# In the full attentions the value projections change places with the turns of normed rows

## The chip, the cores and the metric

The kernel runs on one core of a Trainium2 chip. The metric is the time of one execution in microseconds on the device, the median of three runs. A profile was taken of one more execution.

## The reference, cut to what matters

The reference sends x, 32 sequences of 128 rows with 256 columns, through four layers. Each layer adds an attention over a context to x and then a feed-forward net. Layers 0, 1 and 3 have the same form of attention, the "full attention" here (layer 2 has a windowed one):

```
xn = layernorm(x)                                   # rows of 256
q = xn @ Wq.T + bq;  k = ctx @ Wk.T + bk;  v = ctx @ Wv.T + bv      # 16 heads of 16
scores = (q . k * tau + delta) / 4                  # per head, 128 x 128
a = softmax(scores);  x = x + (a . v) @ Wo.T + bo
```

The feed-forward nets (a routed one, one with rounded weights, product keys, a top-2 one) and the windowed attention are not touched by the change.

## The kernel before

`attention` runs three times (a0, a1 and a3 in the names, for layers 0, 1 and 3). A tile t is one sequence of 128 rows with all 16 heads; four tiles make a group g, and u is the tile's place in its group (t = 4g + u, 32 tiles, 8 groups). Queries and keys are projected for a whole group (512 columns), half of the features at a time; values for two tiles at a time; the normed rows of two tiles at a time are turned (transposed by TensorE against the identity), since the query projection wants features on the partitions.

Each engine has its program written out in order; semaphores tie them together. Nothing plans or reorders. TensorE's program for a tile t (function `tile` under `@block.tensor`) is:

1. `scores` of tile t+1 (L517, 32 matmuls on 32 rows each), which wait until the exponentials of tile t-1 have left the score banks;
2. `values_over_sums` of tile t-1 (L560);
3. `first_filler`: one piece of projection or turning for a later group;
4. `turned_scores` of tile t (L534, 32 matmuls), which wait until VectorE has taken both maxima of tile t+1 (L686) out of the score banks, and has added the maxima of tile t to its queries;
5. `turned_maxima` of tile t+1 (L544);
6. `second_filler`: another such piece;
7. `output_rows` of tile t-2 (L570).

The score banks are thus used in turn by the scores (read by VectorE's maxima) and the turned scores (read by ScalarE's exponentials, `exps`, L342).

The fillers, by u: 0, queries of the next group (L490), first half in the first filler and second half in the second; 1, keys of the next group (L475) in the same way; 2 and 3, in the first filler the turns of the normed rows of the group after next (`columns`, L484, four transposes), in the second filler a value projection (`values`, L498, eight matmuls). Groups 6 and 7 have no group after next, so their first filler is empty in u = 2 and 3; group 7 has of the values only those of u = 2. All fillers write one PSUM bank, `ps_m`, and each waits until ScalarE has evicted what the filler before wrote there.

ScalarE's program for a tile: the eviction of the second filler of the tile before, the eviction of output rows (L349), in some tiles the norm of two tiles of the group after next (L318) or work on the rounded weights of layer 1 (`integers`, in a1), the eviction of the first filler (values L337, turned rows L324), and the exponentials. VectorE: maxima, turning back and dividing (L701, L708), adding maxima (L694), statistics of finished rows (L143, L145); in a0 and a1 it takes the statistics of later rows of x as well in tiles 0 to 7. GpSimd multiplies keys by tau (L433) around u = 1 and 2 and adds rows into x (L440, L444). SP's queue loads the context of group g+2 when values and keys of group g are done.

Of the kernel before, what the change touches and what calls it, by code (L numbers as in the profile page):

```python
# [17 lines left out]
KC = D // P  # L18
# [5 lines left out]
GROUPS = TILES // G  # L24
# [177 lines left out]
def attention(nc, keep, tag, w, inputs, ctxT, following, load_first=False, integers=None, arrival=None, spins=(0, 0)):  # L202

    with ExitStack() as ctx:
# [3 lines left out]
        def sem(name):  # L208
            return keep["semaphore"](f"{tag}_{name}")

        def bank(name):
            return ctx.enter_context(nc.psum_tensor(f"{tag}_ps_{name}", [P, 512], F32))
# [29 lines left out]
        ps_o, ps_m, ps_y, ps_z = bank("o"), bank("m"), bank("y"), bank("z")  # L242
# [6 lines left out]
        k_full, k_taken, k_ready = sem("k_full"), sem("k_taken"), sem("k_ready")  # L249
        xn_ready, xt_full, xt_taken = sem("xn_ready"), sem("xt_full"), sem("xt_taken")  # L250
        q_full, q_taken = sem("q_full"), sem("q_taken")
        v_full, v_taken = sem("v_full"), sem("v_taken")
# [44 lines left out]
        def _(act):  # L297
            def keys(g, c, src):
                n = g * KC + c
                act.wait_ge(k_full, n + 1)  # L300
                if n >= 2:
                    act.wait_ge(k_ready, n - 1)
                for f in range(2):
                    ins = act.activation(kraw[:, c, f, :], src, ACT.Identity, scale=marks[:, 2 + f:3 + f],
                                         bias=bk4[:, f, c:c + 1])
                ins.then_inc(k_taken, 1)
# [15 lines left out]
            def columns(g, n, src):  # L322
                act.wait_ge(xt_full, g * 2 + n + 1)
                act.activation(xnT[:, :, n * 256:(n + 1) * 256], src.rearrange("p (k n) -> p k n", k=KC),  # L324
                               ACT.Copy).then_inc(xt_taken, 1)

            def queries(g, s, c, src):
                act.wait_ge(q_full, g * KC + c + 1)
                for f in range(2):
                    ins = act.activation(qT[:, s, f, c, :], src, ACT.Identity, scale=marks[:, f:f + 1],  # L330
                                         bias=bq4[:, f, c:c + 1])
                ins.then_inc(q_taken, 1)

            def values(g, s, n, src):
                act.wait_ge(v_full, g * 2 + n + 1)
                pairs = v[:, s, n * HEADS:(n + 1) * HEADS, :].rearrange("p a (b e) -> p a b e", b=3)
                act.activation(pairs[:, :, 0:3:2, :], src.rearrange("p (a b e) -> p a b e", b=2, e=DK),  # L337
                               ACT.Copy).then_inc(v_taken, 1)
# [12 lines left out]
            def first_filler(g, u):  # L351
                s, m = g % 2, ps_m[:, :]
                if u == 0 and g + 1 < GROUPS:
                    queries(g + 1, 1 - s, 0, m)
                elif u == 1 and g + 1 < GROUPS:
                    keys(g + 1, 0, m)
                elif u >= 2 and g + 2 < GROUPS:
                    columns(g + 2, u - 2, m)

            def second_filler(g, u):  # L360
                s, m = g % 2, ps_m[:, :]
                if u == 0 and g + 1 < GROUPS:
                    queries(g + 1, 1 - s, 1, m)
                elif u == 1 and g + 1 < GROUPS:
                    keys(g + 1, 1, m)
                elif u == 2:
                    values(g, s, 1, m)
                elif u == 3 and g + 1 < GROUPS:
                    values(g + 1, 1 - s, 0, m)

            def tile(g, u):
                t = g * G + u
                if t:
                    second_filler((t - 1) // G, (t - 1) % G)
                if t >= 3:
                    outputs(t - 3)
                if arrival and t == Arrival.LATE:
                    deviations(2)
                if g + 2 < GROUPS and u in (1, 2):
                    norm(g + 2, u - 1)  # L380
                if integers and g == 3 and u < 3:
                    integers.magnitudes(act, u)
                if integers and 0 <= t - ROUND_FROM < 12:
                    integers.rounded(act, 2 * (t - ROUND_FROM))
                    integers.rounded(act, 2 * (t - ROUND_FROM) + 1)
                first_filler(g, u)
                exps(t)
# [82 lines left out]
        def _(pe):  # L470
            def keys(g, s, c, dst):
                if c == 0:
                    wait_context(pe, g, s)
                for k in range(KC):
                    ins = pe.matmul(dst, wk[:, k, c * P:(c + 1) * P], ctx_t[:, s, k, :], start=(k == 0),  # L475
                                    stop=(k == KC - 1))
                ins.then_inc(k_full, 1)

            def columns(g, n, dst):
                pe.wait_ge(xn_ready, g * 2 + n + 1)  # L480
                for u in (2 * n, 2 * n + 1):
                    for k in range(KC):
                        at = k * 256 + (u % 2) * P
                        ins = pe.transpose(dst[:, at:at + P], xn[:, u, k * P:(k + 1) * P], ident[:, :])  # L484
                ins.then_inc(xt_full, 1)

            def queries(g, c, dst):
                pe.wait_ge(xt_taken, g * 2 + 2)
                for k in range(KC):
                    ins = pe.matmul(dst, wq[:, k, c * P:(c + 1) * P], xnT[:, k, :], start=(k == 0),  # L490
                                    stop=(k == KC - 1))
                ins.then_inc(q_full, 1)

            def values(s, n, dst):
                for u in range(2):
                    at = (2 * n + u) * P
                    for k in range(KC):
                        ins = pe.matmul(dst[:, u * D:(u + 1) * D], ctx_t[:, s, k, at:at + P], wv[:, k, :],  # L498
                                        start=(k == 0), stop=(k == KC - 1))
                ins.then_inc(v_full, 1)  # L500
# [72 lines left out]
            def columns_taken(g, n):  # L573
                pe.wait_ge(xt_taken, g * 2 + n + 1)

            def first_filler(g, u):
                m, more = ps_m[:, :], g + 1 < GROUPS
                if u == 0 and more:
                    if g == 0:
                        columns_taken(0, 1)  # L580
                    else:
                        pe.wait_ge(v_taken, 2 * g + 1)
                    queries(g + 1, 0, m)
                elif u == 1 and more:
                    pe.wait_ge(q_taken, (g + 1) * KC + 2)
                    keys(g + 1, (g + 1) % 2, 0, m)
                elif u == 2 and g + 2 < GROUPS:
                    pe.wait_ge(k_taken, (g + 1) * KC + 2)
                    columns(g + 2, 0, m)
                elif u == 3 and g + 2 < GROUPS:  # L590
                    pe.wait_ge(v_taken, 2 * g + 2)
                    columns(g + 2, 1, m)

            def second_filler(g, u):
                s, m, more = g % 2, ps_m[:, :], g + 1 < GROUPS
                if u == 0 and more:
                    pe.wait_ge(q_taken, (g + 1) * KC + 1)
                    queries(g + 1, 1, m)
                elif u == 1 and more:
                    pe.wait_ge(k_taken, (g + 1) * KC + 1)  # L600
                    keys(g + 1, 1 - s, 1, m)
                elif u == 2:
                    if g + 2 < GROUPS:
                        columns_taken(g + 2, 0)
                    elif more:
                        pe.wait_ge(k_taken, (g + 1) * KC + 2)
                    else:
                        pe.wait_ge(v_taken, 2 * g + 1)
                    values(s, 1, m)
                elif u == 3 and more:  # L610
                    if g + 2 < GROUPS:
                        columns_taken(g + 2, 1)
                    else:
                        pe.wait_ge(v_taken, 2 * g + 2)
                    values(1 - s, 0, m)

            def tile(g, u):
                t = g * G + u
# [2725 lines left out]
```

## Time and profile before

| what | value |
|---|---|
| median of 3 runs | 3050.51 us (3050.44 to 3053.91) |
| profiled execution | 3049.06 us, its span 3047.2 us |
| TensorE matmuls (PE) | 2832.8 us busy, 93% of the span |
| VectorE (DVE) | 2095.7 us, 69% |
| ScalarE (ACT) | 1158.2 us, 38% |
| GpSimd (POOL) | 984.4 us, 32% |

The span reaches from the first to the last instruction; the execution's time has 1.86 us around it. The three full attentions lie at about 28 to 290, 826 to 1090 and 2598 to 2858 us, so they make up a quarter of the span; the long stretch between the second and the third belongs to the product keys. Busy shares are means over stages with different limits, so they say little on one stage; a stage is read from its own timeline and from what its waits end on. In a timeline, instructions of one line that follow one another stand in one row, with the count behind the x; "us" reaches from the first start to the last end, and as matmuls overlap, the next row starts before that end.

### The profile page before, as it was taken

Reading aid. Unit: us, or ns where it says so; the run is one execution under the profiler, and the core shown is the slowest. Engines: PE = TensorE matmul, PEld = TensorE weight load, DVE = VectorE, ACT = ScalarE, POOL = GpSimd, SP = SyncE. Lnnn points to the kernel's source line nnn. Section 1 sums busy time; section 2 is a strip of 40 time slices with the busy share of each in tenths; the row PEclk is TensorE's granted clock in tenths of the full one; section 3 lists DMA queues with packets and bytes.
Section 4 is the critical chain, followed back from the end, with each engine's and each line's share of the span. In section 5 each row is a group of like instructions: output and inputs, shape, how many; then the busy total and the mean of one; then the engine's idle time right before and its main releaser. Section 6 shows DMA issues by size and latency. Waiting matters only on the chain. (4 is left out here: it accounts for less than half of the span.)

```text
span 3047.2 us, 60068 instructions
## 1 busy us (share of the span) xinstructions
PE 2832.8 (93%) x23998; PEld 2131.4 (70%) x23998; DVE 2095.7 (69%) x6103; ACT 1158.2 (38%) x1771; POOL 984.4 (32%) x1024
## 2 busy tenths in 40 slices
PE   8997999999899979897999999999999997999798
PEld 5665766566566656576888888888888885666565
DVE  5766355200277789666999899999999997567534
ACT  5654221222366669554222222222222220655532
POOL 1332000133223322000444444444444444223255
PEclk9999999999999999999999999999999997999899
DMA  4011120234401000402120000000000001100077
GB/s 143 30 43 32 55 74 21 65 100 127 128 29 43 16 12 1 145 22 94 51 82 5 5 5 5 5 6 5 5 5 5 5 5 43 60 29 30 17 228 227
DMA packets 112675, 152.90 MB, mean 50 GB/s; under 512 B 14608, under 2 KB 92688, under 8 KB 112016
## 3 DMA queue, kind: packets, MB, share of 16 engines
q1 hardware_dynamic: 100608, 126.89, 12.5%
q0 software_dynamic: 10752, 21.11, 2.7%
q8 instruction: 194, 3.18, 0.4%
q10 hardware_dynamic: 1040, 1.05, 0.1%
q14 instruction: 81, 0.66, 0.1%
HBM read 102.76 MB, written 46.27 MB: 49 GB/s over the span
## 5 line engine op out<-in xcount | busy, mean ns | idle before, releaser
L2226 POOL TENSOR_TENSOR pk_hisig<-pk_hihot,pk_sigs 128x512 f16<-128x512 f16 x512 | 520.3, 1043 | 660.1 <-DVE pk_hihot L2502 658.6
L2324 PE MATMUL pk_ps<-X,dw_downT 128*128 128x256 f32 x2048 | 479.0, 385 | 0.0
L2370 PE MATMUL pk_ps<-ew_up,pk_act_h 128*128 128x256 f32 x2048 | 459.1, 383 | 1.7 <-DVE pk_act_h L2490 1.7
L2370 PEld LDWEIGHTS pk_ps<-ew_up,pk_act_h 128*128 128x128 f32 x2048 | 388.9, 191 | 56.9 <-issue 2.0
L2324 PEld LDWEIGHTS pk_ps<-X,dw_downT 128*128 128x128 f32 x2048 | 380.2, 191 | 59.7 <-issue 14.8
L2234 ACT ACTIVATE pk_act_h<-pk_ps 128x512 f32<-128x512 f32 x256 | 152.8, 597 | 544.3 <-PE pk_ps L2324 544.3
L2503 DVE TENSOR_TENSOR pk_lohot<-pk_iota_h,pk_ps 128x1024 f16<-128x1024 f16 x256 | 310.1, 1212 | 0.0
L686 DVE TENSOR_REDUCE a_mx<-a_ps_s 128x8 f32<-128x1024 f32 x192 | 226.3, 1221 | 116.4 <-PE a_ps_s L517 101.9
L342 ACT ACTIVATE a_pT<-a_ps_s 128x2048 f32<-128x2048 f32 x96 | 180.2, 1877 | 122.0 <-PE a_ps_s L534 121.9
L2490 DVE TENSOR_TENSOR pk_act_h<-pk_act_h,pk_ps 128x512 f32<-128x512 f32 x256 | 171.3, 679 | 61.3 <-PE pk_ps L2354 61.3
L444 POOL TENSOR_TENSOR X<-a_y,a_tmp 128x256 f32<-128x256 f32 x96 | 69.8, 727 | 405.8 <-ACT a_y L349 404.4
L534 PE MATMUL a_ps_s<-a_qT,a_kT 32*128 32x128 f32 x3072 | 112.7, 283 | 59.2 <-DVE a_mx L686 59.2
L534 PEld LDWEIGHTS a_ps_s<-a_qT,a_kT 32*128 32x128 f32 x3072 | 94.4, 186 | 104.4 <-DVE a_mx L686 103.8
L2354 PEld LDWEIGHTS pk_ps<-pk_hisig,pk_lohot 128*128 128x128 f16 x4096 | 140.7, 99 | 37.1 <-DVE pk_act_h L2490 11.4
L2354 PE MATMUL pk_ps<-pk_hisig,pk_lohot 128*128 128x64 f16 x4096 | 145.7, 195 | 17.4 <-POOL pk_hisig L2226 7.2
L1512 DVE TENSOR_TENSOR ro_tmp<-ro_ps,ro_b 128x256 f32<-128x256 f32 x28 | 11.9, 424 | 190.0 <-PE ro_ps L1473 190.0
L517 PEld LDWEIGHTS a_ps_s<-a_kT,a_qT 32*128 32x128 f32 x3072 | 94.5, 186 | 46.5 <-issue 35.8
L694 DVE TENSOR_TENSOR a_qT<-a_ps_z,a_qT 128x512 f32<-128x512 f32 x96 | 66.4, 691 | 86.3 <-PE a_ps_z L544 86.3
L517 PE MATMUL a_ps_s<-a_kT,a_qT 32*128 32x128 f32 x3072 | 112.7, 283 | 11.7 <-ACT a_pT L342 8.2
L2502 DVE TENSOR_TENSOR pk_hihot<-pk_iota_h,pk_ps 128x256 f16<-128x256 f16 x256 | 105.6, 412 | 20.4 <-ACT pk_sigs L2275 20.4
L2313 PE MATMUL pk_ps<-pk_wm,pk_xb 128*128 128x512 f32 x256 | 117.0, 600 | 1.6 <-issue 1.6
L1145 PE MATMUL sh_ps<-sh_xnT,sh_w 128*128 128x512 f32 x256 | 117.7, 606 | 0.7 <-issue 0.7
(419 smaller groups left out, 5172.3 us busy)
## 6 DMA issues: line engine op xcount, KB each, us to landing
ro_w<-in_L_W SPq DMA_DIRECT2D x16, 1024.0 KB, 7.2
sent<-pk_zero SPq DMA_DIRECT2D x3, 3072.0 KB, 11.1
mo_xb<-sent SPq DMA_DIRECT2D x36, 256.0 KB, 4.4
made<-mo_yb SPq DMA_DIRECT2D x36, 256.0 KB, 3.8
i_ctx_t<-in_ctxT SPq DMA_DIRECT2D x16, 512.0 KB, 3.6
i_side<-in_side SPq DMA_DIRECT2D x16, 512.0 KB, 4.6
row_dram<-sh_row SPq DMA_DIRECT2D x8, 512.0 KB, 3.0
sum_dram<-sh_new SPq DMA_DIRECT2D x8, 512.0 KB, 2.9
```

The lines of the kernel that those rows point to most:

```text
L342: act.activation(pT[:, :, :], ps_s[:, :, :, :].rearrange("p r h n -> p (r h) n"), ACT.Exp).then_inc(p_taken, 1)
L517: ins = pe.matmul(ps_s[:, r, 2 * c + f, :], qT[row, s, f, c, at], kT[row, s, f, c, at], start=True, stop=True, skip_group_check=True)
L534: ins = pe.matmul(ps_s[:, r, 2 * c + f, :], kT[row, s, f, c, at], qT[row, s, f, c, at], start=True, stop=True, skip_group_check=True)
L686: dve.tensor_reduce(mx[:, :, 0:4, c:c + 1].rearrange("p f r a -> p r (f a)"), ps_s[:, :, 2 * c:2 * c + 2, :], AX_X, ALU.max).then_inc(max_ ...
L1145: ins = pe.matmul(main.bank(f"up{c}")[:, :], w1[:, k, c * P:(c + 1) * P], xnT[:, k, g * GT:(g + 1) * GT], start=(k == 0), stop=(k == KC - 1))
L2226: ins = pool.tensor_tensor(hisig[:, buf, n, :, :, :], hi, sig2.broadcast_to([P, TP, 2, ECH]), ALU.mult)
L2234: hid.take(act.activation(act_h[:, p % 2, 2 * c:2 * c + 2, :], hid.bank(f"h{c}")[:, :].rearrange("p (c n) -> p c n", c=2), ACT.Gelu), f"h{c}")
L2324: ins = pe.matmul(hid.bank(f"h{c}")[:, j * 2 * P:(j + 1) * 2 * P], downT[:, k, e * P:(e + 1) * P], XT[:, p, k, :], start=(k == 0), stop=(k ...
L2354: ins = pe.matmul(wts.bank(f"w{b}")[:, j * 2 * ECH:(j + 1) * 2 * ECH], lohot[:, buf, j, :], hisig[:, buf, n, j, :, :].rearrange("p r c -> ...
L2370: ins = pe.matmul(tail.bank("y")[:, 0:D], act_h[:, p % 2, c, s * P:(s + 1) * P], up[:, c, :], start=(c == 0), stop=(c == ECH - 1))
L2490: wts.take(dve.tensor_tensor(hv, hv, wts.bank(f"w{b}")[:, :].rearrange("p (j c) -> p c j", c=ECH), ALU.mult), f"w{b}")
L2503: ins = dve.tensor_tensor(lohot[:, buf, :, :], *against(0, P))
```

## The change

In tiles with u = 2 and u = 3 the two fillers change places: the value projection stands ahead of the turned scores, and the turns of normed rows behind the turn of the maxima. ScalarE's evictions change places with them. The waits for `ps_m` are rewritten for the new order: a value projection now waits for the filler of the tile before, the turns for the eviction of the values (`v_taken`). What is computed, and the number of instructions, stays. Layer 2's attention and the nets stay as they were.

```diff
--- before.py
+++ after.py
@@ -354,8 +354,10 @@
                     queries(g + 1, 1 - s, 0, m)
                 elif u == 1 and g + 1 < GROUPS:
                     keys(g + 1, 0, m)
-                elif u >= 2 and g + 2 < GROUPS:
-                    columns(g + 2, u - 2, m)
+                elif u == 2:
+                    values(g, s, 1, m)
+                elif u == 3 and g + 1 < GROUPS:
+                    values(g + 1, 1 - s, 0, m)
 
             def second_filler(g, u):
                 s, m = g % 2, ps_m[:, :]
@@ -363,10 +365,8 @@
                     queries(g + 1, 1 - s, 1, m)
                 elif u == 1 and g + 1 < GROUPS:
                     keys(g + 1, 1, m)
-                elif u == 2:
-                    values(g, s, 1, m)
-                elif u == 3 and g + 1 < GROUPS:
-                    values(g + 1, 1 - s, 0, m)
+                elif u >= 2 and g + 2 < GROUPS:
+                    columns(g + 2, u - 2, m)
 
             def tile(g, u):
                 t = g * G + u
@@ -574,22 +574,25 @@
                 pe.wait_ge(xt_taken, g * 2 + n + 1)
 
             def first_filler(g, u):
-                m, more = ps_m[:, :], g + 1 < GROUPS
+                s, m, more = g % 2, ps_m[:, :], g + 1 < GROUPS
                 if u == 0 and more:
-                    if g == 0:
-                        columns_taken(0, 1)
-                    else:
-                        pe.wait_ge(v_taken, 2 * g + 1)
+                    columns_taken(g + 1 if g else 0, 1)
                     queries(g + 1, 0, m)
                 elif u == 1 and more:
                     pe.wait_ge(q_taken, (g + 1) * KC + 2)
                     keys(g + 1, (g + 1) % 2, 0, m)
-                elif u == 2 and g + 2 < GROUPS:
-                    pe.wait_ge(k_taken, (g + 1) * KC + 2)
-                    columns(g + 2, 0, m)
-                elif u == 3 and g + 2 < GROUPS:
-                    pe.wait_ge(v_taken, 2 * g + 2)
-                    columns(g + 2, 1, m)
+                elif u == 2:
+                    if more:
+                        pe.wait_ge(k_taken, (g + 1) * KC + 2)
+                    else:
+                        pe.wait_ge(v_taken, 2 * g + 1)
+                    values(s, 1, m)
+                elif u == 3 and more:
+                    if g + 2 < GROUPS:
+                        columns_taken(g + 2, 0)
+                    else:
+                        pe.wait_ge(v_taken, 2 * g + 2)
+                    values(1 - s, 0, m)
 
             def second_filler(g, u):
                 s, m, more = g % 2, ps_m[:, :], g + 1 < GROUPS
@@ -599,20 +602,9 @@
                 elif u == 1 and more:
                     pe.wait_ge(k_taken, (g + 1) * KC + 1)
                     keys(g + 1, 1 - s, 1, m)
-                elif u == 2:
-                    if g + 2 < GROUPS:
-                        columns_taken(g + 2, 0)
-                    elif more:
-                        pe.wait_ge(k_taken, (g + 1) * KC + 2)
-                    else:
-                        pe.wait_ge(v_taken, 2 * g + 1)
-                    values(s, 1, m)
-                elif u == 3 and more:
-                    if g + 2 < GROUPS:
-                        columns_taken(g + 2, 1)
-                    else:
-                        pe.wait_ge(v_taken, 2 * g + 2)
-                    values(1 - s, 0, m)
+                elif u >= 2 and g + 2 < GROUPS:
+                    pe.wait_ge(v_taken, 2 * g + u)
+                    columns(g + 2, u - 2, m)
 
             def tile(g, u):
                 t = g * G + u
```

## Rows read from the trace of the kernel before

**Rows 1.** The page, part 5, the scores and turned scores on TensorE.

```profile
L534 PE MATMUL a_ps_s<-a_qT,a_kT 32*128 32x128 f32 x3072 | 112.7, 283 | 59.2 <-DVE a_mx L686 59.2
...
L517 PE MATMUL a_ps_s<-a_kT,a_qT 32*128 32x128 f32 x3072 | 112.7, 283 | 11.7 <-ACT a_pT L342 8.2
```

**Rows 2.** The maxima's tile: who waited for it (us in all, times).

```profile
  PE a_ps_s L534: 59.2, 54
```

**Rows 3.** TensorE's timeline, first attention: start, us, line, times, [idle before].

```profile
124.20 1.17 PE L517 MATMUL a_ps_s<-a_kT,a_qT 32*128 32x128 f32 x32
125.31 1.08 PE L560 MATMUL a_ps_o<-a_pT,a_v 128*32 128x128 f32 x32
126.32 0.66 PE L484 MATMUL a_ps_m<-ident,a_xn 128*128 128x128 f32 x4
127.86 1.17 PE L534 MATMUL a_ps_s<-a_qT,a_kT 32*128 32x128 f32 x32 [0.88 <-DVE a_mx L686]
128.96 0.44 PE L544 MATMUL a_ps_z<-ident,a_mx 128*128 128x128 f32 x2
129.24 1.89 PE L498 MATMUL a_ps_m<-a_wv,i_ctx_t 128*128 128x256 f32 x8
130.97 1.03 PE L570 MATMUL a_ps_y<-a_wo,a_oT 128*128 128x256 f32 x4
131.92 1.17 PE L517 MATMUL a_ps_s<-a_kT,a_qT 32*128 32x128 f32 x32
...
134.04 1.98 PE L490 MATMUL a_ps_m<-a_xnT,a_wq 128*128 128x512 f32 x4
135.95 1.17 PE L534 MATMUL a_ps_s<-a_qT,a_kT 32*128 32x128 f32 x32
```

**Rows 4.** The same stretch in the timeline of all engines.

```profile
125.44 2.36 DVE L686 TENSOR_REDUCE a_mx<-a_ps_s 128x8 f32<-128x1024 f32 x2 [1.63 <-PE a_ps_s L517]
...
129.10 1.88 ACT L342 ACTIVATE a_pT<-a_ps_s 128x2048 f32<-128x2048 f32 x1 [1.49 <-PE a_ps_s L534]
...
131.35 0.18 DVE L145 BATCH_NORM_AGGREGATE MV<-a_bst 128x2 f32<-128x6 f32 x1
...
137.40 1.87 ACT L342 ACTIVATE a_pT<-a_ps_s 128x2048 f32<-128x2048 f32 x1
```

**Rows 5.** Timeline of all engines, last group of the first attention.

```profile
264.63 1.17 PE L534 MATMUL a_ps_s<-a_qT,a_kT 32*128 32x128 f32 x32 [1.47 <-DVE a_mx L686]
...
265.87 1.88 ACT L342 ACTIVATE a_pT<-a_ps_s 128x2048 f32<-128x2048 f32 x1 [4.40 <-PE a_ps_s L534]
...
267.80 1.17 PE L517 MATMUL a_ps_s<-a_kT,a_qT 32*128 32x128 f32 x32 [0.76 <-ACT a_pT L342]
```

**Rows 6.** TensorE's timeline, tiles 2 and 3 of the first and second attention.

```profile
47.99 1.17 PE L517 MATMUL a_ps_s<-a_kT,a_qT 32*128 32x128 f32 x32
...
52.67 1.17 PE L534 MATMUL a_ps_s<-a_qT,a_kT 32*128 32x128 f32 x32 [1.91 <-DVE a_mx L686]
...
54.05 3.58 PE L498 MATMUL a_ps_m<-a_wv,i_ctx_t 128*128 128x256 f32 x8
...
66.20 1.17 PE L517 MATMUL a_ps_s<-a_kT,a_qT 32*128 32x128 f32 x32
...
845.70 1.17 PE L517 MATMUL a_ps_s<-a_kT,a_qT 32*128 32x128 f32 x32
...
850.40 1.17 PE L534 MATMUL a_ps_s<-a_qT,a_kT 32*128 32x128 f32 x32 [1.92 <-DVE a_mx L686]
...
862.23 1.17 PE L517 MATMUL a_ps_s<-a_kT,a_qT 32*128 32x128 f32 x32
```

**Rows 7.** Busy time by stretches: length, engines (PE first), PEclk, DMA share, GB/s.

```profile
55.00:56.00 1.00, 1.00 (x4) 0.81 (x3) 0.97 (x4) 0.79 (x1) 0.00 (x0) 0.50 0.00 0
```

**Rows 8.** Timeline of all engines, around the product of keys on POOL.

```profile
146.06 2.36 POOL L433 TENSOR_TENSOR a_kT<-a_kraw,i_side 128x1024 f32<-128x1024 f32 x1 [3.88 <-ACT a_kraw L304]
...
146.55 2.15 DVE L708 TENSOR_TENSOR a_rows_o<-a_turned,a_rden 128x256 f32<-128x256 f32 x1
```

## The prediction

> **What bounds the kernel now.** I read the page first, part 5: the turned scores (L534) and the scores (L517) of the three full attentions are the matmuls ahead of which TensorE stands idle, and the turned scores wait for VectorE's maxima [rows 1]. The view of the maxima's tile then says how often: 54 waits, 59.2 us in all [rows 2]. 54 is 45 + 9: per attention 15 tiles whose first filler is the turns of normed rows or nothing while values come later (u=2 and u=3 of groups 0 to 6, u=2 of group 7), and 3 others (tile 0 and the first two of group 7). So I read one such tile in TensorE's timeline [rows 3]. Scores start at 124.20, values over sums at 125.31, the turns at 126.32; the turned scores can't start before 127.86, with 0.88 idle; then come the value projections, 1.73 until the next matmul, and output rows; the next scores start at 131.92. The tile takes 7.72 us, of which TensorE's instructions fill all but that gap. The reader is to see in the tile behind it that queries, 1.91 us long in the same place, leave no gap at all.
>
> What else could set the tile's end is read in the same stretch with all engines [rows 4]: the maxima run 125.44 to 127.80, which is what the gap ends on; the exponentials start at 129.10, 1.24 behind the start of the turned scores, and take 1.88, to 130.98. The next scores need them, and start 0.94 later, so now they are hidden behind value projections and output rows. The last group shows what happens where they are not [rows 5]: turned scores at 264.63, exponentials 265.87 to 267.75, scores at 267.80 after 0.76 idle. From the start of the turned scores to the next scores nothing is shorter than 1.24 + 1.88 + 0.05 = 3.17.
>
> **The change part by part.** No instruction is added or removed; in u=2 and u=3 the 8 value matmuls and the 4 turns (and their two ScalarE evictions) change places. Queues other than PE and ACT keep their order. SP's load of the group after next waits for the second value projection of a group, which now ends about 2.9 us sooner (4.0 behind the scores, not 6.9): at nothing, as a load can only come earlier by it.
>
> First gap. Ahead of the turned scores TensorE now has 1.11 + 1.01 of scores and values over sums, then the value projections. Those take 1.73 up to output rows [rows 3]; up to 32-row matmuls it may be more: four output matmuls, half as many columns, take 0.95 up to the scores (131.92 less 130.97), 0.09 over half of 1.73. The bounds are 1.73 and the 1.91 of queries, which stream as many columns (4 x 512 for 8 x 256) in just this place. I take 1.73 + 0.09 = 1.82, since its rows are the same matmul form. The turned scores then start 2.12 + 1.82 = 3.94 behind the scores, not 3.66, and no longer wait for the maxima (3.66), which have 0.28 to spare.
> The Trainium skill's "TensorEngine Tiling (Array Packing)", section Key Properties, says that changing the tiling mode drains TensorE. A whole drain would hold the turned scores until the last value matmul's end (1.89 behind the first start, as the row of these eight matmuls has it), and the sum below would be 37 x 0.07 = 2.6 us less; the row with output matmuls ahead of scores shows a switch at 0.09, so the trace agrees that it costs, and with less than a whole drain.
>
> Second gap. Behind the turned scores (1.10, from 127.86 to 128.96) TensorE now has the turn of the maxima (0.28), four turns (4 x 0.14 by the two of the maxima, 0.56) and output rows (0.95): 2.89. That no longer covers 3.17, so the exponentials set the end of the tile, with 0.28 idle ahead of the scores. This is where a part of the gain stops: without it the tile would be 6.83 long.
>
> The tile: 3.94 + 3.17 = 7.11 against 7.72, a gain of 0.61 (0.70 and 0.52 at the bounds of the switch).
>
> ScalarE. The eviction of the values (0.60) now stands ahead of the exponentials. It can start when the values are done (about 4.05) and is over at 4.65; the exponentials can't start before 3.94 + 1.24 = 5.18, so nothing. The turns wait for it as they share the bank; they come at about 5.3. The eviction of the turns goes behind the exponentials, over some 0.6 into the next tile, where its bank is wanted at 2.12. If the cover is gone, the exponentials follow the eviction directly, as behind the queries [rows 4]: 137.40 is 1.45 behind 135.95, not 1.24, and each tile loses 0.21.
>
> VectorE. It ends its tile 3.67 behind the start of the turned scores (131.53 less 127.86) [rows 4], so at 7.61; its next maxima may start 1.24 into the next tile, at 8.35. Hidden, with 0.74 left. In tiles 2, 3, 6 and 7 of the first two attentions it carries statistics as well. In tile 2 the maxima come late, and the turned scores start 4.70 behind the scores in the second attention [rows 6]. They stay there, values or not; what follows is now 3.17 instead of 4.06. The next tile is as the others, 7.11. So tiles 2 and 3 take 4.70 + 3.17 + 7.11 = 14.98 against 862.23 - 845.70 = 16.53: a gain of 1.55. For tiles 6 and 7, with the same load on VectorE, I take the same.
>
> The clock. In the first attention tiles 2 and 3 take 66.20 - 47.99 = 18.21 [rows 6], 1.68 more than the same tiles of the second: the eight value matmuls last 3.58 instead of 1.89, and the granted clock is 0.50, the 1.2 GHz level [rows 7]. TensorE had just been idle for 1.91; it would now be idle for 0.76 (4.70 less 3.94). I take the fall as gone: 1.55 + 1.68 = 3.23; the ends are 1.55 and 3.23. That a gap of 1.92 in the second attention brought no fall makes this uncertain.
>
> The sum: of 45 tiles 37 are regular, 37 x 0.61 = 22.6; the two pairs of the second attention and one of the first, 3 x 1.55 = 4.65; the first pair of the first, 3.2. Together 30.5 us. The profiled execution took 3049.06 around a span of 3047.2, so 3018.6; the median of the runs is 1.45 above it, 3050.51, so 3020.0. With the switch at its ends: 37 x 0.52 + 7 = 26 and 37 x 0.70 + 8.5 = 34.
>
> **The rivals.**
> The exponentials late. The eviction ahead of them delays each by up to 0.21, or the switch costs more than its bound. For it: behind queries they start at the eviction's end. Against: two evictions of 0.73 there, one of 0.60 here. 37 x 0.40 + 8 x 0.7 = 20 us: 3030.
> No second limit. If output rows and turns stretched over the exponentials or these came sooner, the tile would be 6.83: 45 x 0.88 = 40 us: 3011. Against: rows 5 show that the scores start 0.05 behind the exponentials.
> VectorE takes the place. Its product with the reciprocals takes 2.15 instead of about 0.4 where GpSimd's product of keys lies beside it [rows 8]. If the shifted tiles met that in u=2 or u=3, VectorE would be 1.74 later, 1.0 over its slack of 0.74, and a tile would take some 0.7 longer than forecast, all of its gain: 3050, no change. Against: the keys' product in u=2 is started by the tile before, and the product with the reciprocals comes later than now, not sooner.
> The clock falls more often. The tiles lose a gap of 0.88 and get one of 0.28 at another place; should the half level then be granted in tiles where it is not now, each fall costs 1.69 by the 3.58 against 1.89. From 18 falls on (30.5 / 1.69) the change doesn't gain; at one in each attention group, 24, it is 3060, slower by 0.3%. Against: the last group, with gaps of 1.47 and 0.76 in each tile, keeps its durations (1.17 for the scores [rows 5]).
> The Trainium skill's "TensorE: Matmul & The Clock Gate", section Part 1, says that activity releases the throttle and idling brings it back, which speaks against this rival too; the fall in the first attention agrees, the second, without a fall behind the same gap, doesn't settle it.
>
> **How the numbers follow.** The forecast 0.77; exponentials late 0.13; no second limit 0.02; VectorE 0.05; clock 0.03. A change of under 0.2% (6.1 us) is about what a measurement of this kernel can't tell from none. Faster is 0.77 + 0.13 + 0.02 = 0.92; same 0.05; slower 0.03. The range is 3015.0 to 3030.0: below, the switch at its cheap end and 1 us for what is left (34 + 1.5); above, the exponentials late. What it leaves out is less than 0.2.
>
> **What would show it.** In the changed profile: regular tiles of 7.1 from scores to scores; value matmuls (L498) between values over sums and turned scores; the idle time of L534 behind the maxima down from 59.2 to some 13 (the 9 other waits and the first tile of four pairs); L517 waiting for the exponentials in some 45 tiles more than now, about 0.3 each; tile 2 of the first attention with eight value matmuls at 1.89. Wrong would be: turned scores that still wait for the maxima in regular tiles, exponentials over 1.3 behind the turned scores, or scores that start more than 0.1 behind the exponentials.

## The result, and the profile after

The changed kernel takes 3027.18 us (median of 4 runs, 3022.56 to 3029.39) against 3052.21 (4 runs, 3050.44 to 3055.29): ratio 0.9917, 95% interval 0.9906 to 0.9929, 25 us less. The forecast was 30.5 us less than the 3050.51 known then, so 3020.0, in a range from 3015.0 to 3030.0. The profiled execution took 3026.22 us around a span of 3024.4.

The page's part 5 for the two matmuls that [rows 1] shows (columns as there; the program's lines behind L600 have moved up by 8, those of the scores haven't):

```profile
L517 PE MATMUL a_ps_s<-a_kT,a_qT 32*128 32x128 f32 x3072 | 114.1, 285 | 28.4 <-ACT a_pT L342 24.9
...
L534 PE MATMUL a_ps_s<-a_qT,a_kT 32*128 32x128 f32 x3072 | 112.7, 283 | 12.0 <-DVE a_mx L678 12.0
```

The idle time ahead of the turned scores fell from 59.2 to 12.0 us, and that ahead of the scores rose from 11.7 to 28.4: 47 us went in one place, and 17 came back in another. Who waited for the maxima, in the view of their tile, answers [rows 2]:

```profile
  PE a_ps_s L534: 12.0, 12
```

12 waits for 54: of the 45 changed tiles only the first tiles of the four pairs with additional statistics still wait, 0.57 or 0.29 each. TensorE's timeline of a regular tile, which answers [rows 3] (start, us, line, count, idle before):

```profile
119.72 1.17 PE L517 MATMUL a_ps_s<-a_kT,a_qT 32*128 32x128 f32 x32 [0.33 <-ACT a_pT L342]
120.82 1.08 PE L560 MATMUL a_ps_o<-a_pT,a_v 128*32 128x128 f32 x32
121.83 1.99 PE L498 MATMUL a_ps_m<-a_wv,i_ctx_t 128*128 128x256 f32 x8
123.76 1.17 PE L534 MATMUL a_ps_s<-a_qT,a_kT 32*128 32x128 f32 x32
...
125.14 0.60 PE L484 MATMUL a_ps_m<-ident,a_xn 128*128 128x128 f32 x4
125.57 1.03 PE L570 MATMUL a_ps_y<-a_wo,a_oT 128*128 128x256 f32 x4
126.93 1.17 PE L517 MATMUL a_ps_s<-a_kT,a_qT 32*128 32x128 f32 x32 [0.33 <-ACT a_pT L342]
```

And the other engines in the same stretch, as in [rows 4]:

```profile
120.96 2.36 DVE L678 TENSOR_REDUCE a_mx<-a_ps_s 128x8 f32<-128x1024 f32 x2 [0.73 <-PE a_ps_s L517]
...
123.86 0.60 ACT L337 ACTIVATE a_v<-a_ps_m 128x512 f32<-128x512 f32 x1 [3.44 <-PE a_ps_m L498]
...
125.00 1.88 ACT L342 ACTIVATE a_pT<-a_ps_s 128x2048 f32<-128x2048 f32 x1 [0.54 <-PE a_ps_s L534]
...
127.25 0.18 DVE L145 BATCH_NORM_AGGREGATE MV<-a_bst 128x2 f32<-128x6 f32 x1
```

The value projections (121.83) stand ahead of the turned scores, which start 4.04 behind the scores with no wait. The maxima had ended at 123.32, so they are off the path. The eviction of the values (123.86 to 124.46) is over 0.54 before the exponentials start, 1.24 behind the turned scores. They end at 126.88, and the next scores start at 126.93, after 0.33 idle. The tile takes 7.21, not 7.72. VectorE is through at 127.43, and its next maxima start 1.24 behind 126.93, so it has 0.7 to spare.

### The profile page after: what moved, and what is told of

It is laid out like the page before. It is cut to its first block and busy times, and to the rows that moved or that the text cites. A ratio compares the mean times of both kernels' runs of the same rounds, so it can differ in the third digit from the quotient of the medians.

```text
span 3024.4 us, 60068 instructions
## 1 busy us (share of the span) xinstructions
PE 2838.9 (94%) x23998; PEld 2131.7 (70%) x23998; DVE 2096.8 (69%) x6103; ACT 1149.9 (38%) x1771; POOL 985.3 (33%) x1024
## 5 line engine op out<-in xcount | busy, mean ns | idle before, releaser
L444 POOL TENSOR_TENSOR X<-a_y,a_tmp 128x256 f32<-128x256 f32 x96 | 69.9, 728 | 379.1 <-ACT a_y L349 377.7
L517 PE MATMUL a_ps_s<-a_kT,a_qT 32*128 32x128 f32 x3072 | 114.1, 285 | 28.4 <-ACT a_pT L342 24.9
L433 POOL TENSOR_TENSOR a_kT<-a_kraw,i_side 128x1024 f32<-128x1024 f32 x32 | 75.5, 2362 | 134.4 <-ACT a_kraw L304 134.4
```

Of the source, the lines that this page charges most:

```text
L517: ins = pe.matmul(ps_s[:, r, 2 * c + f, :], qT[row, s, f, c, at], kT[row, s, f, c, at], start=True, stop=True, skip_group_check=True)
```

## The experiments

Two theories are set against each other. Theory A, which the prediction held: in a changed tile the turned scores start when the maxima *and* TensorE's work ahead of them are done, and the next scores start 3.17 later, by the exponentials, or when TensorE is through, whichever is later. Rival B: something else ends the tile (evictions, VectorE, the sum of TensorE's work). Times are medians; the kernel before took 3051.7 to 3053.3 in these rounds.

**The changed kernel again.**

> The changed kernel as it is, for its spread and as the one to compare with. Both theories: regular tiles of 7.21 us from scores to scores, ratio to the kernel before 0.990 to 0.994. If the half clock in the first attention (tile 2 before, tile 0 after) hangs on where an execution happens to stand and not on the order of work, it lies in tile 0, in tile 2 or in neither here, worth 1.6 us; if it hangs on the order, it is in tile 0 again.

3028.43 us, ratio 0.9926 (0.9913 to 0.994); regular tiles (changed ones without additional statistics on VectorE) 7.21. No tile of the three attentions shows the half clock.

**The exponentials in four pieces**, in the changed kernel and in the kernel before:

```diff
-                act.activation(pT[:, :, :], ps_s[...], ACT.Exp).then_inc(p_taken, 1)
+                for r in range(4):
+                    ins = act.activation(pT[:, 4 * r:4 * r + 4, :], ps_s[:, r, :, :], ACT.Exp)
+                ins.then_inc(p_taken, 1)
```

> The changed kernel with the exponentials of a tile in four pieces of 512 columns instead of one of 2048; each tile's exponentials should last 2.1 us instead of 1.88. Theory A (exponentials set the end of the changed tiles): regular tiles of u=2 and 3 grow by just as much, 7.4 for 7.21, tiles of u=0 and 1 stay at 8.41; in all some 10 us slower than the changed kernel. Theory B (TensorE or evictions set the end): the tiles stay within 0.05, the whole within 3 us.

> The kernel before with the exponentials in four pieces, as in the changed kernel with pieces; they last 2.06 there instead of 1.88. Theory A (before, the exponentials end 0.94 ahead of the next scores and don't set the end of a regular tile): regular tiles stay at 7.72, tiles of the last group grow from 6.82 to 7.01; 2 us slower in all, ratio 0.999 to 1.002. Theory B (they set the end in both kernels, or pieces cost in another way): regular tiles 7.9, 8 to 10 us slower, ratio 1.003.

Timelines of all engines, a regular tile each (L518 is the scores, L535 the turned scores, L343 the exponentials), first in the changed kernel, then in the kernel before:

```profile
120.31 1.17 PE L518 MATMUL a_ps_s<-a_kT,a_qT 32*128 32x128 f32 x32 [0.51 <-ACT a_pT L343]
...
124.35 1.17 PE L535 MATMUL a_ps_s<-a_qT,a_kT 32*128 32x128 f32 x32
...
125.59 2.06 ACT L343 ACTIVATE a_pT<-a_ps_s 128x512 f32<-128x512 f32 x4 [0.54 <-PE a_ps_s L535]
...
127.71 1.17 PE L518 MATMUL a_ps_s<-a_kT,a_qT 32*128 32x128 f32 x32 [0.52 <-ACT a_pT L343]
```

```profile
123.82 1.17 PE L518 MATMUL a_ps_s<-a_kT,a_qT 32*128 32x128 f32 x32
...
127.48 1.17 PE L535 MATMUL a_ps_s<-a_qT,a_kT 32*128 32x128 f32 x32 [0.88 <-DVE a_mx L687]
...
128.72 2.06 ACT L343 ACTIVATE a_pT<-a_ps_s 128x512 f32<-128x512 f32 x4 [1.49 <-PE a_ps_s L535]
...
131.54 1.17 PE L518 MATMUL a_ps_s<-a_kT,a_qT 32*128 32x128 f32 x32
```

The pieces last 2.06 in both, 0.18 longer. Changed, the tile grows from 7.21 to 7.40 (127.71 less 120.31), and the kernel to 3036.76, 8.3 us over the changed one. Before, the tile stays at 7.72 (131.54 less 123.82) and the ratio is 1.001 (1.0001 to 1.002); the attentions lose 2.05 us in all, in the few tiles whose end the exponentials set before as well (6.82 to 7.01 in the last group). So the exponentials set the end of a regular tile after the change and not before it: theory A.

**Output rows in the first gap**, once in place of the values (on the kernel before), once behind them (on the changed kernel). The edit is the same:

```diff
                 first_filler(g, u)
+                if u >= 2:
+                    output_rows(t - 2)
                 turned_scores(t)
...
-                if t >= 2:
+                if t >= 2 and u < 2:
                     output_rows(t - 2)
```

> The kernel before, with the output rows of u=2 and u=3 moved ahead of the turned scores instead of the value projections. Theory A (a tile ends 3.17 behind the start of the turned scores, by the exponentials, or when TensorE is through, whichever is later; turned scores start when maxima and fillers are done): 1.11 + 1.01 + 0.10 + 0.43 + 0.96 = 3.61, so the turned scores start with the maxima at 3.66; behind them 1.10 + 0.28 + 1.82 = 3.20, tile 6.86, 0.35 less than with values ahead; some 13 us faster than the changed kernel, ratio to before 0.986 to 0.989. Theory B (it is the value projections in the first gap that count, the end is set by the evictions on ScalarE): the tile stays at 7.2 or more, the ratio at 0.992 or above.

> The changed kernel with the output rows of u=2 and u=3 ahead of the turned scores as well, behind the value projections: too much in the first gap. Theory A: turned scores 4.04 + 0.87 = 4.91 behind the scores, regular tiles 4.91 + 3.17 = 8.08, 0.36 longer than in the kernel before; 12 to 18 us slower than before, ratio 1.003 to 1.006, although no work is added. Theory B (the end of a tile is set by the sum of TensorE's work): 7.2, no change against the changed kernel, ratio 0.992.

TensorE's timeline, a regular tile, first on the kernel before, then on the changed one:

```profile
111.32 1.17 PE L517 MATMUL a_ps_s<-a_kT,a_qT 32*128 32x128 f32 x32
...
114.97 1.17 PE L534 MATMUL a_ps_s<-a_qT,a_kT 32*128 32x128 f32 x32
...
116.35 1.89 PE L498 MATMUL a_ps_m<-a_wv,i_ctx_t 128*128 128x256 f32 x8
118.17 1.17 PE L517 MATMUL a_ps_s<-a_kT,a_qT 32*128 32x128 f32 x32
```

```profile
114.95 1.17 PE L517 MATMUL a_ps_s<-a_kT,a_qT 32*128 32x128 f32 x32
...
119.85 1.17 PE L534 MATMUL a_ps_s<-a_qT,a_kT 32*128 32x128 f32 x32
...
123.02 1.17 PE L517 MATMUL a_ps_s<-a_kT,a_qT 32*128 32x128 f32 x32 [1.19 <-ACT a_pT L342]
```

On the kernel before, the turned scores start 3.65 behind the scores, just when the maxima end, and the tile takes 6.85: theory A's 6.86. The kernel takes 3020.54, ratio 0.9899 (0.9884 to 0.9914), 8 us less than the changed one, not 13. Nearly all of the rest is lost in the last two tiles, where output rows ahead of the turned scores delay the last exponentials: there 6.12 lie between the turned scores, 4.18 in the changed kernel, and from the last scores to the last turned scores it is 9.77 for 8.22, 1.55 in each of three attentions. On the changed kernel the gap is overfilled: turned scores at 4.90, the tile 8.07, 1.19 idle ahead of the scores, and the kernel slower than before, 3072.29, ratio 1.0062 (1.0045 to 1.0079), with not one instruction more. That is 20 us over the kernel before, 2 more than the forecast's upper end; 16.4 of it lie in the three attentions (775.73 us from first scores to last turned scores, 759.28 in the second profile of the kernel before), the rest in code that the edit leaves as it was. The work given to TensorE, which is the same in all of these, doesn't set the tile.

The rows of the first kernel also show where the forecast went wrong: there the value matmuls, behind the turn of the maxima (matmuls on the whole array), take 1.82 up to the next 32-row matmul (116.35 to 118.17); ahead of the turned scores of the changed kernel, behind values over sums (matmuls on a tile of 32 columns), they take 1.93 (121.83 to 123.76).

**Values over sums behind the first filler**, in all tiles of the changed kernel:

```diff
+                first_filler(g, u)
                 if t:
                     values_over_sums(t - 1)
-                first_filler(g, u)
                 turned_scores(t)
```

> The changed kernel with values over sums behind the first filler instead of ahead of it, in all tiles. Theory A (the turned scores start late by 0.10 as the first weight load of the values is not hidden behind values over sums, and by 0.09 for the switch to 32-row matmuls behind them): turned scores at 3.85 to 4.04 behind the scores in u=2 and 3; in u=0 and 1 the second filler no longer waits 0.2 to 0.3 for the eviction of the first, tiles of 8.1 to 8.2 for 8.41; in all 8 to 18 us faster than the changed kernel. Theory B (VectorE is close behind: turning back starts 0.4 later, and its maxima come late): turned scores wait for the maxima, tiles of u=2 and 3 at 7.3 or more, no gain or up to 10 us slower.

```profile
115.19 1.18 PE L517 MATMUL a_ps_s<-a_kT,a_qT 32*128 32x128 f32 x32 [0.32 <-ACT a_pT L342]
116.30 2.00 PE L498 MATMUL a_ps_m<-a_wv,i_ctx_t 128*128 128x256 f32 x8
118.22 1.08 PE L560 MATMUL a_ps_o<-a_pT,a_v 128*32 128x128 f32 x32
119.23 1.17 PE L534 MATMUL a_ps_s<-a_qT,a_kT 32*128 32x128 f32 x32
...
122.40 1.17 PE L517 MATMUL a_ps_s<-a_kT,a_qT 32*128 32x128 f32 x32 [0.33 <-ACT a_pT L342]
...
130.49 1.17 PE L517 MATMUL a_ps_s<-a_kT,a_qT 32*128 32x128 f32 x32
```

The turned scores stay at 4.04 (115.19 to 119.23): the values now follow 32-row matmuls, and take 1.92. So neither neighbour hides the cost, and the regular tiles of u=2 and 3 gain nothing. Those of u=0 fall from 8.41 to 8.09 (130.49 less 122.40), since the eviction of queries is over sooner, and the first weight load of their second half no longer waits for it (0.30 in the changed kernel). 3012.14 us, ratio 0.9877 (0.9862 to 0.9892), 16 us less than the changed kernel, 13.0 of them in the attentions (720.40 for 733.37); VectorE didn't get in the way of regular tiles. In one place the half clock did: in the first tile of the last group of the second attention, behind a wait of 1.78, the turned scores take 2.02 instead of 1.17 and the tile 7.97 instead of 7.13 (TensorE's timeline). The changed kernel with output rows ahead has the same fall in the same tile, 7.91.

```profile
1028.24 2.02 PE L534 MATMUL a_ps_s<-a_qT,a_kT 32*128 32x128 f32 x32 [1.78 <-DVE a_mx L678]
```

**Both: output rows ahead on the kernel before, sums behind the first filler.**

> The kernel before with output rows ahead of the turned scores in u=2 and u=3, and values over sums behind the first filler in all tiles. Theory A: the two gains add, tiles of 6.86 in u=2 and 3 and 8.08 in u=0 and 1; 3002 to 3008 us, ratio 0.983 to 0.986. Theory B (VectorE is in the way where tiles are short and its input comes late): tiles of u=2 and 3 at 7.0 or more, 3012 or above.

3007.46 us, ratio 0.9854 (0.9837 to 0.987), within the forecast, but by another way: tiles of u=2 and 3 take 6.96, not 6.86.

```profile
114.09 1.17 PE L517 MATMUL a_ps_s<-a_kT,a_qT 32*128 32x128 f32 x32
...
116.79 1.13 PE L570 MATMUL a_ps_y<-a_wo,a_oT 128*128 128x256 f32 x4
117.85 1.17 PE L534 MATMUL a_ps_s<-a_qT,a_kT 32*128 32x128 f32 x32
...
121.05 1.17 PE L517 MATMUL a_ps_s<-a_kT,a_qT 32*128 32x128 f32 x32
```

Output rows behind values over sums take 1.06 up to the turned scores (116.79 to 117.85), for 0.95 in [rows 3]: again 0.1 where whole-array matmuls follow tiled ones. There is one such step more in this order.

**By place**: output rows ahead in u=2 and 3 (not in the last tile), sums behind the filler in u=0 and 1 alone.

```diff
+                if u < 2:
+                    first_filler(g, u)
                 if t:
                     values_over_sums(t - 1)
-                first_filler(g, u)
+                if u >= 2:
+                    first_filler(g, u)
+                    if t + 1 < TILES:
+                        output_rows(t - 2)
                 turned_scores(t)
...
-                if t >= 2:
+                if t >= 2 and (u < 2 or t + 1 == TILES):
                     output_rows(t - 2)
```

> The kernel before with output rows ahead of the turned scores in u=2 and u=3 (but not in the very last tile), and values over sums behind the first filler in u=0 and u=1 alone. Theory A (each change from tiled matmuls to whole-array ones costs 0.10 where the first weight load has nothing to hide behind; with sums behind the turns in u=2 and 3 there was one more): turned scores at 3.66, tiles of 6.86 in u=2 and 3, of 8.08 in u=0 and 1; 3.7 us less than the kernel with both everywhere, and 3 us less for the last tiles: 2999 to 3003 us, ratio 0.982 to 0.985. Theory B (the 0.10 there came from VectorE's input, not from TensorE): tiles of u=2 and 3 stay at 6.96, time at 3006 to 3009.

```profile
114.64 1.17 PE L517 MATMUL a_ps_s<-a_kT,a_qT 32*128 32x128 f32 x32
...
118.29 1.17 PE L534 MATMUL a_ps_s<-a_qT,a_kT 32*128 32x128 f32 x32
...
121.49 1.17 PE L517 MATMUL a_ps_s<-a_kT,a_qT 32*128 32x128 f32 x32
...
129.57 1.17 PE L517 MATMUL a_ps_s<-a_kT,a_qT 32*128 32x128 f32 x32
```

6.85 (u=2, and u=3 likewise) and 8.08: both parts at their full size, with the turned scores at 3.65. 2997.45 us, 1.5 below the forecast's low end, ratio 0.982 (0.9807 to 0.9834): it beats both kernels, and does so with the order of the kernel before in its fillers.

**The kernel before again.**

> The kernel before as it is, for a second profile of it. Theory A (the half clock in the first attention hangs on where an execution stands): tile 2 of the first attention takes 8.76 as in the second attention, or 10.4 with the half clock again, or another of the first tiles is long. Theory B (it hangs on the order of work, here the gap of 1.91): 10.4 in tile 2 again. Ratio 1.000, within 0.001.

Ratio 0.9999 (0.9989 to 1.0008). TensorE's timeline of tile 2 of the first attention:

```profile
47.62 1.17 PE L517 MATMUL a_ps_s<-a_kT,a_qT 32*128 32x128 f32 x32
...
53.88 3.33 PE L498 MATMUL a_ps_m<-a_wv,i_ctx_t 128*128 128x256 f32 x8
...
58.00 1.17 PE L517 MATMUL a_ps_s<-a_kT,a_qT 32*128 32x128 f32 x32
```

The tile takes 10.38, for 10.43 in the first profile, with the value matmuls at 3.33. But in the profile of the kernel before with pieces, whose tile 2 has the same gap (1.87), it was tile 0 that was long (9.72), and tile 2 took 8.71. So the gap alone doesn't bring the fall; whether the earlier fall in tile 0 spared tile 2 there isn't shown.

## Why the prediction was right, and where it was short

The mechanism was right and the time lies in the range, though near its upper end, by a term that was sized too small; 25 us came where 30.5 were forecast. By its steps:

**First gap.** The wait for the maxima went in regular tiles, as forecast. The term that was short is that of the value projections: 1.82 was taken, 1.93 measured, so the turned scores start at 4.04 and not at 3.94, and the tile takes 7.21 and not 7.11: 37 x 0.10 = 3.7 us. The sum priced the step from whole-array to 32-row matmuls behind the values (0.09) and not the step ahead of them. A narrow window on the first value matmul shows it, first in the changed kernel, then in the kernel before, in timelines of all engines (PEld is the weight load):

```profile
121.83 0.30 PEld L498 LDWEIGHTS a_ps_m<-a_wv,i_ctx_t 128*128 128x128 f32 x2 [0.20 <-issue]
121.83 0.48 PE L498 MATMUL a_ps_m<-a_wv,i_ctx_t 128*128 128x256 f32 x1
```

```profile
129.13 0.30 PEld L498 LDWEIGHTS a_ps_m<-a_wv,i_ctx_t 128*128 128x128 f32 x2
129.24 0.38 PE L498 MATMUL a_ps_m<-a_wv,i_ctx_t 128*128 128x256 f32 x1
```

Before, behind the turn of the maxima, the weights load 0.11 ahead of the matmul, beside the matmul before it. Behind values over sums they load only when the matmul is due, and the first matmul's record lasts 0.10 longer (0.48 for 0.38). The experiments show the same 1.92 to 1.93 behind two tiled kinds and 1.82 behind a whole-array one; that the weight load causes the whole of it, and not another part of the step, isn't shown apart. The upper bound, 1.91 from queries in the same place, came nearest, 0.02 short; the choice of the middle was the error. That row has the step ahead in it, and should have been taken.
The Trainium skill's rule ("TensorEngine Tiling (Array Packing)", Key Properties) that changing the tiling mode drains TensorE is borne out in part: behind the values the turned scores start 0.06 before the last value matmul's recorded end (121.83 + 1.99 less 123.76), where output rows, on the whole array as the values are, start 0.16 before it (129.24 + 1.89 less 130.97, [rows 3]); so a change of mode waits longer, but by these records not for a whole drain. The step into the whole array costs about as much as the step out (0.10 and 0.09), and the prediction had weighed the rule on the step out alone.

**Second gap.** Right, as a number too: 1.24, 1.88 and 0.05, idle 0.33 for 0.28. The split exponentials show that it is they that set the end. The rival of late exponentials (1.45 behind the turned scores) and that without a second limit (no idle time ahead of the scores) are both out by these figures.

**ScalarE and VectorE.** Right in regular tiles. Once VectorE did take the place: in the first tile of group 7 of the second attention the turned scores start 3.96 behind the scores and not 3.65, 0.31 in all, as VectorE's limiting of the rounded weights takes 1.22 and not 0.66 ahead of the maxima. Timelines of all engines, first in the changed kernel (the scores start at 1038.37), then in the kernel before:

```profile
1038.73 0.72 POOL L444 TENSOR_TENSOR X<-a_y,a_tmp 128x256 f32<-128x256 f32 x1 [5.78 <-ACT a_y L349]
1038.79 1.22 DVE L878 TENSOR_SCALAR bq_up<-bq_up 128x2048 bf16<-128x2048 bf16 x1
...
1042.32 1.18 PE L534 MATMUL a_ps_s<-a_qT,a_kT 32*128 32x128 f32 x32 [1.77 <-DVE a_mx L678]
```

```profile
1056.64 0.66 DVE L886 TENSOR_SCALAR bq_up<-bq_up 128x2048 bf16<-128x2048 bf16 x1
```

This is the forecast's third rival, VectorE slow beside GpSimd, on another instruction. In the changed order the limiting starts 0.06 behind GpSimd's addition into x (L444); before, no GpSimd instruction lies beside it. All four profiles with 1.22 have this overlap. In the changed kernel with pieces the limiting starts 0.12 ahead of the addition: it keeps its 0.66, and the addition takes 1.12 for 0.73. Shorter tiles alone don't bring it: at 6.85 a tile the limiting takes 0.66.

**Tiles 2 and 3, 6 and 7.** Their gain was 1.47 and 1.46 (15.06 and 14.77 us in the second attention) for 1.55, by the same 0.1 in the second tile.

**The clock.** Right in tile 2, but not shown to be the change's doing, and it may be luck. Tile 2 of the first attention went from 10.43 to 7.85, as forecast; but in this execution the half clock stood in tile 0 of the first attention and in the start of the second, in work that the change leaves as it was. TensorE's timeline, and the granted clock by stretches, columns as in [rows 7]:

```profile
31.53 1.89 PE L517 MATMUL a_ps_s<-a_kT,a_qT 32*128 32x128 f32 x32
33.35 2.89 PE L490 MATMUL a_ps_m<-a_xnT,a_wq 128*128 128x512 f32 x4
```

```profile
33.00:35.00 2.00, 2.00 (x10) 0.97 (x7) 1.51 (x2) 0.00 (x0) 0.00 (x0) 0.50 0.01 4
818.00:819.00 1.00, 1.00 (x9) 0.67 (x11) 0.08 (x1) 0.51 (x1) 0.00 (x0) 0.50 1.01 385
```

Tile 0 took 9.53 for 7.90 in the first attention, and the second's start lost 1.1. The changed kernel again had neither, so a fall of this size comes and goes between executions of one program. Both profiles of the kernel before have it in tile 2, and neither of the changed kernel has it there; with so few profiles, what the change does to it stays open, as does what decides where the fall comes. No regular tile of the eleven profiles shows it, so nothing supports the rival of more frequent falls there.

**The sum** for the profiled execution: 30.5 less 3.7 (values), 0.3 (second tiles of pairs), 1.6 and 1.1 (clock), 0.3 (VectorE) leaves 23.5; without the two falls it is 26.2. From the first scores to the last turned scores the three attentions took 254.97, 253.38 and 250.97 before and 246.39, 246.31 and 243.37 after, 23.25 less; in the changed kernel again, without the falls, 733.37 in all, 25.95 less. The rest of the span was 2287.9 before and 2288.3 after, and 2291.3 and 2292.9 in the second profile of each: untouched code that differs by 3 to 5 us between executions, as much as the whole error of the forecast.

## What to carry to other kernels

A gap in front of a matmul is worth filling only up to what ends it (here the maxima, 3.65 behind the scores): work beyond that pushes the chain behind it, and the same instructions gave 6.85, 7.21, 7.72 or 8.07 us a tile by their order alone. Choose the piece by its length for the gap, and look which wait ends the tile once the gap is full. Price a moved run of matmuls with both of its neighbours, from the row that stands in the same place.

## What the runs showed of the hardware

Eight whole-array matmuls of 256 columns behind row- or column-tiled ones took 0.10 us more than behind whole-array ones (1.92 and 1.93 for 1.82), and four transposes 0.06 more (0.66 for 0.60); the first weight load then starts with its matmul and not 0.11 ahead of it. 32-row matmuls behind whole-array ones start 0.09 later than another whole-array one does (1.82 for 1.73 behind the values). One Exp over 2048 columns took 1.88 us, four over 512 took 2.06. A VectorE instruction of 0.66 us took 1.22 where it started 0.06 behind a GpSimd addition; where it started first, the addition took 1.12 for 0.73. The granted clock fell to 0.50, the 1.2 GHz level, in tile 0 or 2 of an attention or in the first tile of its last group, at a price of 0.8 to 1.7 us, in tile 0 in one execution and not in another of the same program.
